# Attention block on one core: all large products of four slots in one step, all value products in the other, and result stores issued behind the copies

## What is computed

```python
xf = x.reshape(16, 1024, 512)
h = group_norm(xf, groups=32, eps=1e-6) * norm_scale + norm_bias   # mean, variance over tokens and 16 channels
q, k, v = split(h @ qkv_w + qkv_b, 3)                              # 512 x 1536
# q, k, v are reshaped (bs * 8 heads, length, 64) WITHOUT a transpose: a "head" is
# 128 consecutive tokens, and each token gives 8 positions of 64 channels (1024 positions)
a = softmax((q * s) @ (k * s).T) @ v                               # s = 64 ** -0.25, 1024 x 1024 per head
out = xf + (a.reshape(16, 1024, 512) @ proj_w + proj_b)
```

## Time and profile before

| | |
|---|---|
| median of 3 runs | 3506.1 us (3504.74 to 3506.66) |
| the profiled execution, its own time | 3506.26 us |
| its span, first to last instruction | 3504.5 us |
| VectorE busy | 2782.3 us (79%) |
| ScalarE busy | 2062.2 us (59%) |
| GpSimd busy | 1626.9 us (46%) |
| transfers | 646.87 MB, 185 GB/s; the copies' queue 76.5% of 16 engines |
| granted TensorE clock, mean | 0.998 |

### The profile page before, as it was taken

One profiled execution on the slowest core, in us unless ns is written; L12 is line 12 of the kernel. 1 busy time (PEld: TensorE's weight loads), 2 busy tenths in 40 slices (PEclk: granted clock), 3 DMA queues, 4 the chain that ended last, 5 costly groups with the idle time before them and its releaser, 6 DMA issues.

```text
span 3504.5 us, 67790 instructions
## 1 busy us (share of the span) xinstructions
PE 3454.0 (99%) x24640; PEld 2515.0 (72%) x24640; DVE 2782.3 (79%) x3473; ACT 2062.2 (59%) x3985; POOL 1626.9 (46%) x2762
## 2 busy tenths in 40 slices
PE   6999999999999999999999999999999999999998
PEld 4777777777777777777777777777777777777775
DVE  4878878888788787887888788887878878888776
ACT  5566566565565665655656656556556566565563
POOL 4454444454444444444544444445454444444452
PEclk9999999999999999999999999999999999999999
DMA  4777778777787878777777787877777778777777
GB/s 126 191 182 190 187 186 191 181 190 184 187 192 182 191 181 191 186 187 189 183 190 188 182 193 179 195 183 186 190 183 190 184 187 191 181 191 185 178 180 171
DMA packets 255707, 646.87 MB, mean 185 GB/s; under 512 B 73872, under 2 KB 73872, under 8 KB 255376
## 3 DMA queue, kind: packets, MB, share of 16 engines
q1 hardware_dynamic: 254224, 638.35, 76.5%
q10 hardware_dynamic: 1152, 4.19, 0.3%
HBM read 71.84 MB, written 33.55 MB: 30 GB/s over the span
## 4 chain that ended last, share of the span: by engine, by line
PE 91%; POOL 3%; ACT 2%; DVE 1%; issue 1%; SPq 1%; DMA 0%; POOLq 0%; ACTq 0%
PE pv_ps L399 26%; PE s_ps L369 22%; PE c_ps L439 7%; PE c_ps L440 6%; PE c_ps L441 6%; PE c_ps L422 4%; PE c_ps L450 4%; PE c_ps L452 3%; PE c_ps L424 3%; PE c_ps L423 3%; PE c_ps L451 3%; PE pv_ps L380 2%; PE s_ps L472 2%; ACT staged L519 1%; ACT probs L501 1%
## 5 line engine op out<-in xcount | busy, mean ns | idle before, releaser
L632 DVE TENSOR_REDUCE neg_max<-s_ps 128x1 f32<-128x1024 f32 x1024 | 1204.6, 1218 | 642.0 <-PE s_ps L369 642.0
L501 ACT ACTIVATE probs<-s_ps,neg_max 128x1024 f32<-128x1024 f32 x1024 | 1143.6, 1117 | 938.8 <-DVE neg_max L632 935.4
L615 DVE STREAM_TRANSPOSE turned<-probs 128x1024 f32<-128x1024 f32 x1024 | 1231.2, 1226 | 40.5 <-ACT probs L501 6.0
L399 PE MATMUL pv_ps<-probs_t,v 128*64 128x256 f32 x8192 | 999.9, 386 | 9.6 <-DMA probs_t<-turned 9.6
L399 PEld LDWEIGHTS pv_ps<-probs_t,v 128*64 128x64 f32 x8192 | 544.6, 137 | 347.0 <-issue 117.6
L439 PE MATMUL c_ps<-h_hi,w_hi 128*128 128x256 f32 x2048 | 606.7, 296 | 10.3 <-POOL h_lo L742 6.4
L440 PE MATMUL c_ps<-h_lo,w_hi 128*128 128x256 f32 x2048 | 579.3, 283 | 0.0
L441 PE MATMUL c_ps<-h_hi,w_lo 128*128 128x256 f32 x2048 | 579.1, 283 | 0.0
L519 ACT ACTIVATE staged<-c_ps,qk_bias 64x256 f32<-64x256 f32 x1024 | 479.7, 468 | 18.2 <-PE c_ps L441 4.7
L439 PEld LDWEIGHTS c_ps<-h_hi,w_hi 128*128 128x128 f32 x2048 | 391.1, 191 | 102.6 <-issue 96.6
L755 POOL CAST qh_e<-staged 128x256 fp32r<-128x256 f32 x256 | 102.4, 400 | 648.8 <-ACT staged L519 648.8
(11 more groups left out here) (71 smaller groups left out, 5171.3 us busy)
## 6 DMA issues: line engine op xcount, KB each, us to landing
probs_t<-turned SPq DMA_DIRECT2D x4096, 128.0 KB, 2.3
x_res<-in_x SPq DMA_DIRECT2D x128, 256.0 KB, 2.9
result<-x_res SPq DMA_DIRECT2D x128, 256.0 KB, 2.0
x_next<-in_x SPq DMA_DIRECT2D x120, 256.0 KB, 2.9
probs_t<-in_L_conv_qkv_w ACTq DMA_DIRECT2D x4, 768.0 KB, 8.7
turned<-in_x SPq DMA_DIRECT2D x4, 512.0 KB, 13.1
probs_t<-in_L_conv_proj_w ACTq DMA_DIRECT2D x4, 256.0 KB, 13.8
v_bias<-in_L_conv_qkv_b SPq DMA_DIRECT2D x1, 256.0 KB, 16.9
```

The costliest lines, as they stand in the source:

```text
L399: last = nc.tensor.matmul(pv_ps[side][CH * par:CH * (par + 1), 0, :], v_sb[:, ring_of(i, parity), CH * chunk:CH * (chunk + 1)], p_t[:, par ...
L501: nc.scalar.activation(probs[k % 2][:, :], s_ps[k % 2][:, :], ACT.Exp, bias=neg_max[:, k % 4:k % 4 + 1], accum_out=row_sum[:, (k // HALF) ...
L615: nc.vector.transpose(dst, probs[k % 2][:, :].rearrange("p (k b j) -> p k b j", k=CHUNKS, b=QUADS)).then_inc(probs_turned, 1)
L632: nc.vector.tensor_reduce(neg_max[:, k % 4:k % 4 + 1], s_ps[k % 2][:, :], AX.X, ALU.max, negate=True).then_inc(max_ready, 1)
```

## The change

Numbers of lines in the text are those of the kernel before. The change:

- TensorE: steps take turns. In a step with k % 4 == 0: scores of two slots, all large units of four slots (`LARGE`), the inverse transposes (`SPREAD_LAG` 8). In the other: scores of two slots and all 32 value matmuls (`ATTEND_LAG` 10). The small work stands before the third large unit (`SMALL_BEFORE`), that of slot 46 behind the value matmuls.
- The large work is laid out anew: both value units at m = 0; query/key, projection, query/key at 4 and 12; four query/key units at 8. The query/key units come in the order of tiles 0, 1, 4, 5, 2, 3, 6, 7 (0 to 3 queries, 4 to 7 keys). Statistics slots move to multiples of four.
- ScalarE, VectorE and GpSimd take their work in the new order. GpSimd runs one block of work for four slots, with `widen_inverse` of the current half as its last item but one.
- SyncE: `store` moves from m = 4 and 12, ahead of `move_half`, to m = 6 and 14, behind it. In both kernels SyncE issues it.

```diff
-STAT_SLOTS = [1, 9, 13, 17, 25, 29, 37, 41]
-STAT_STEPS = [4, 12, 14, 20, 28, 30, 38, 42]
+STAT_SLOTS = [4, 8, 12, 20, 24, 28, 36, 40]
+STAT_STEPS = [8, 12, 20, 24, 28, 36, 40, 42]
 AGGREGATE_SLOT = 42
-GROUP_MEAN_SLOT = 45
-GROUP_VAR_SLOT = 47
-AFFINE_SLOT = 47
-SPLIT_SLOT = 2
+GROUP_MEAN_SLOT = 44
+GROUP_VAR_SLOT = 46
+
+LARGE = {0: [("v", 0), ("v", 1)], 4: [("qk", 0), ("proj", 0), ("qk", 1)],
+         8: [("qk", 2), ("qk", 3), ("qk", 4), ("qk", 5)], 12: [("qk", 6), ("proj", 1), ("qk", 7)]}
+QK_TILES = [0, 1, 4, 5, 2, 3, 6, 7]
+SMALL_BEFORE = 2
 MOVE_LAG = 4
-WIDEN_LAG = 7
-ATTEND_LAG = 9
+SPREAD_LAG = 8
+ATTEND_LAG = 10
 EVAC_LAG = 12
...
@@ sync
             def slot(b, k):
-                if k == 0:
-                    load_x_tile(b, 0)
-                if k % 16 == 4:
-                    store(b, 2 * (k // 16) - 2)
-                if k % 16 == 12:
-                    store(b, 2 * (k // 16) - 1)
                 if k % HALF == MOVE_LAG % HALF:
                     move_half(b, k)
+                if k % 16 == 6:
+                    store(b, 2 * (k // 16) - 2)
+                if k % 16 == 14:
+                    store(b, 2 * (k // 16) - 1)
                 if k % 16 == 7:
                     load_residual(b, 2 * (k // 16) - 1)
                 if k % 16 == 15:
                     load_residual(b, 2 * (k // 16))
+                if k == 1:
+                    load_x_tile(b, 0)
                 if k - 2 in STAT_SLOTS[:-1]:
                     load_x_tile(b, STAT_SLOTS.index(k - 2) + 1)
...
@@ tensor
-                if k % 2 == 0 and k > 0 and small_taken(b, k - 1)[0]:
-                    pe.wait_ge(*small_taken(b, k - 1)[1:])
+                if k >= 2 and small_taken(b, k - 2)[0]:
+                    pe.wait_ge(*small_taken(b, k - 2)[1:])
...
                 if not before_start(b):
-                    pe.wait_ge(probs_ready, SPB * b + k)
+                    pe.wait_ge(probs_ready, SPB * b + k + 1)
...
-            def slot(b, k):
+            def step(b, k):
                 s = SPB * b + k
-                if k % 2 == 0 and within(s, N_SLOTS):
+                if within(s, N_SLOTS):
                     scores(b, k)
                     scores(b, k + 1)
-                large(b, k)
-                small(b, k)
-                if k % HALF == ATTEND_LAG % HALF and within(s - ATTEND_LAG, N_SLOTS):
-                    spread_inverse(b, k)
-                    attend(b, k, 0)
-                if k % HALF == (ATTEND_LAG + 2) % HALF and within(s - ATTEND_LAG - 2, N_SLOTS):
-                    attend(b, k - 2, 1)
+                if k % HALF == 0:
+                    for i, (kind, n) in enumerate(LARGE[k % 16]):
+                        if i == SMALL_BEFORE:
+                            small(b, k)
+                        make[kind](b, k, i, n)
+                    if within(s - SPREAD_LAG, N_SLOTS):
+                        spread_inverse(b, k)
+                else:
+                    if within(s - ATTEND_LAG, N_SLOTS):
+                        attend(b, k)
+                    small(b, k)
...
@@ scalar
                 if within(s, N_SLOTS):
                     softmax_exp(b, k)
+                if k % 16 == 8:
+                    stage_qk(b, k, 0)
+                if within(s, N_SLOTS):
                     softmax_exp(b, k + 1)
-                if small_unit(k + 1)[0] == "stats" and within(b + 1, BATCHES):
-                    copy_x(b, k + 1)
-                for slot in (k, k + 1):
-                    kind, n, _ = large_unit(slot)
-                    if kind == "qk" and within(made_pair(b, slot), N_PAIRS):
-                        stage_qk(b, slot, n)
+                if k % 16 == 4 or k % 16 == 12:
+                    stage_qk(b, k, 0)
+                if small_unit(k)[0] == "stats" and within(b + 1, BATCHES):
+                    copy_x(b, k)
+                if k % 16 == 4 or k % 16 == 12:
+                    stage_qk(b, k, 2)
+                if k % 16 == 8:
+                    stage_qk(b, k, 1)
+                    stage_qk(b, k, 2)
+                    stage_qk(b, k, 3)
                 if k % 16 == 0 and within(made_pair(b, k), N_PAIRS):
                     norm_x(b, k, 0)
                     norm_x(b, k, 1)
...
@@ vector
                 if within(s, N_SLOTS):
                     turn(b, k)
-                kind, _, part = large_unit(k + 1)
-                if kind == "v" and large_unit(k + 1)[1] == 1:
-                    take_v(b, k + 1)
-                if kind == "proj":
-                    take_proj(b, k + 1)
+                if k % 16 == 0:
+                    take_v(b, k, 0)
                 if within(s, N_SLOTS):
                     turn(b, k + 1)
+                if k % 16 == 0:
+                    take_v(b, k, 1)
+                if k % 16 == 4 or k % 16 == 12:
+                    take_proj(b, k, 1)
...
@@ gpsimd
             def widen_inverse(b, k):
-                n = (k - WIDEN_LAG) // HALF
+                n = k // HALF
...
-            def slot(b, k):
+            def four_slots(b, k):
                 m, pair = k % 16, k // 16
-                if k % HALF == (EVAC_LAG + 1) % HALF:
-                    split_attn(b, (k - 1) // HALF - EVAC_LAG // HALF)
-                if m == SPLIT_SLOT and within(made_pair(b, k), N_PAIRS):
-                    split_h(b, k)
-                kind, n, _ = large_unit(k)
-                if kind == "qk" and within(made_pair(b, k), N_PAIRS):
-                    split_qk(b, k, n)
-                if k % HALF == WIDEN_LAG % HALF:
-                    widen_inverse(b, k)
-                if k == AFFINE_SLOT and within(b + 1, BATCHES):
-                    affine(b)
-                if m == 9:
-                    add_bias(b, 2 * pair - 1)
-                if m == 1:
-                    add_bias(b, 2 * pair - 2)
+                if m == 4 or m == 12:
+                    split_qk(b, k, LARGE[m][0][1])
+                if m == 8:
+                    split_qk(b, k, LARGE[m][0][1])
+                    split_qk(b, k, LARGE[m][1][1])
+                split_attn(b, (k - EVAC_LAG) // HALF)
+                if m == 0:
+                    add_bias(b, 2 * pair - 2)
+                if m == 0 and within(made_pair(b, k), N_PAIRS):
+                    split_h(b, k)
+                if m == 8:
+                    add_bias(b, 2 * pair - 1)
+                if m == 4 or m == 12:
+                    split_qk(b, k, LARGE[m][2][1])
+                if m == 8:
+                    split_qk(b, k, LARGE[m][2][1])
+                    split_qk(b, k, LARGE[m][3][1])
+                widen_inverse(b, k)
+                if k == GROUP_MEAN_SLOT and within(b + 1, BATCHES):
+                    affine(b)
```

More of the change, by code:

```diff
@@ L387, in attend @@
                 i, parity = (n // 2) % 2, (n // 4) % 2
[L388 to L395, removed]
+                for quad in range(QUADS):
+                    pe.wait_ge(moved[n % 2][quad], 64 * (BLOCKS * b + n // 2 + 1))
+                if n % 4 == 0:
+                    pe.wait_ge(v_ready, 2 * (PPB * b + n // 4) + 1)
+                if n % 4 == 2:
+                    pe.wait_ge(v_ready, 2 * (PPB * b + n // 4) + 2)
+                for kt in range(8):
                     chunk = 2 * (kt % 4) + kt // 4
@@ new lines, in attend, with project @@
+                last.then_inc(pv_done, 1)
+            def project(b, k, i, n):
+                h, c = proj_block(b, k, n), bank(k, i)
+                if not within(h, N_BLOCKS):
+                    return
+                if h == 0:
+                    pe.wait_ge(w_ready, 2 * KT)
+                pe.wait_ge(attn_ready, 2 * h + 2)
+                await_bank(pe, b, k, i)
+                for j in range(KT):
+                    a_hi = attn_hi[:, j // 2, (j % 2) * P:(j % 2 + 1) * P]
+                    a_lo = attn_lo[:, j // 2, (j % 2) * P:(j % 2 + 1) * P]
+                    nc.tensor.matmul(c[:, :], a_hi, pw_hi[:, j, :], start=(j == 0), stop=False)
+                    nc.tensor.matmul(c[:, :], a_hi, pw_lo[:, j, :], start=False, stop=False)
+                    last = nc.tensor.matmul(c[:, :], a_lo, pw_hi[:, j, :], start=False, stop=(j == KT - 1))
+                last.then_inc(proj_full, 1)
@@ new lines, in make_qk @@
+            def make_qk(b, k, i, n):
+                g, c, tile = made_pair(b, k), bank(k, i), QK_TILES[n]
+                if not within(g, N_PAIRS):
+                    return
+                if before_start(b) and n == 0:
+                    pe.wait_ge(w_ready, KT)
+                await_bank(pe, b, k, i)
+                for t in range(KT):
+                    if n == 0 and t % 2 == 0:
+                        pe.wait_ge(h_split, 2 * g + t // 2 + 1)
+                    wh, wl = (w[:, t, tile * P:(tile + 1) * P] for w in (w_hi, w_lo))
+                    nc.tensor.matmul(c[:, 0:2 * P], wh, h_hi[:, t, :], start=(t == 0), stop=False)
+                    nc.tensor.matmul(c[:, 0:2 * P], wh, h_lo[:, t, :], start=False, stop=False)
```

(25 more changed lines are left out.)

137 lines of the change are left out of this document (39 added, 98 removed).

## The result

The changed kernel takes 3676.3 us (3674.3 to 3678.9, four runs) against 3506.1: ratio 1.049, interval 1.047 to 1.051. It is slower by 4.9%; 3668 was forecast. Its profiled execution has a span of 3672.6 us.

The account below looks back on a forecast made before the run. Bound: TensorE's matmuls and the changes between its kinds of work. Sum: 3506.3 - 97 + 139 + 26 + 30 + 31 + 12 + 18 + 3 = 3668 us; own range 3610 to 3730, eight in ten 3565 to 3757.

Parts of the forecast that it names:

- The forecast case: The whole kernel: all terms summed come to 3668 us, 4.6% slower; chance 0.56, own range 3610 to 3730.
- Changes removed: TensorE: two fewer changes between kinds of work in each of 256 halves, 0.19 us each, 97 us less.
- The wait at m = 8: Held GpSimd delays ScalarE's third staging, then exponentials and TensorE's scores: 2.19 us in 63 of 64 pairs, 139 us more.
- T: Start of the inverse transposes at the end of step m = 8; scores forecast at T + 7.28, without the wait T + 5.52.
- The bank at m = 4: The second query/key unit waits for the first's bank: 0.3 us in 45 places, 0.7 in 18, 26 us more.
- Once for an image: Statistics at slot 42 (30), affine work behind the held widening (31), variance product behind slot 46's values (12): about 73 us more.
- The clock: TensorE's granted clock falls behind one long stall in six, 1.7 us each: 18 us more, bounds 0 and 107.
- SyncE: SyncE's moved stores: copies start about 1 us late at most twice a pair, covered by slack; 0 us.
- Start and tail: First scores start 0.8 us earlier, last copies come some 3 us later; 3 us more.

Follow-up runs that it names:

- run 3: Run 1's kernel, with ScalarE staging the first query/key unit of m = 4 and 12 between its two exponentials; 3443.1 us, ratio 0.982.
- run 6: Run 3's kernel with the inverse transposes between the two halves of the value matmuls (lag 6), six changes in four slots instead of four; 3512.5 us, ratio 1.002.
- run 1: The changed kernel with SPREAD_LAG 4 instead of 8, so the inverse transposes come four slots earlier; 3469.7 us, ratio 0.990.
- run 2: The changed kernel with ScalarE's third and fourth staging of m = 8 moved behind the exponentials of slots 10 and 11; 3516.2 us, ratio 1.003.
- run 8: The changed kernel with one more GpSimd operation, its result unused, right behind the widening's wait in each half; 3708.6 us, ratio 1.058.
- run 5: The kernel before with only its stores moved to m = 6 and 14, behind the copies; 3513.6 us, ratio 1.0025.
- run 4: The changed kernel with SyncE's stores back at m = 4 and 12, ahead of the copies; 4016.5 us, ratio 1.146.
- run 7: Run 3's kernel with SyncE's stores back at m = 4 and 12, ahead of the copies; 3907.3 us, ratio 1.115.

## Why the prediction was right

The forecast case came in, with its mechanism: 3668 against 3676.3, 162 us added against 170. Point by point:

- **Changes removed, -97.** In run 3 an image takes 210.3 us, of which 1.7 are waits at slots 44 and 46; without them 208.6 against 214.8 before. 6.2 x 16 = 99. The neighbours that no row had shown behave like the others: transposes to scores 0.31 (1720.62 to 1720.93), where transposes to values had 0.34, and a score block ahead of values 1.60 (1720.93 to 1722.53), where one ahead of large work had 1.59. That the 99 are changes and nothing else is inferred from this; run 6, which put two back elsewhere, lost 69.
- **The wait at m = 8, +139.** By the forecast the scores come at T + 7.28, the trace has T + 7.31. Step 10 is 1.80 longer than in run 1. Steps 12 and 28 are 0.42 longer, the forecast's 0.43, and step 60, without an image tile, 0.55; taking 0.55 for slot 44 too, 32 x 2.22 + 31 x 2.35 = 144. Runs 1, 2 and 8 cut it at its first link, cut it at its second, and lengthened it, and the time followed.
- **The bank at m = 4, +26.** 24 step by step (run 3), at the forecast's 0.3 and 0.7 us. The working did not give these two: 6.45 less 5.9 and 6.3 is 0.55 and 0.15, and the 0.15 that brings them to 0.7 and 0.3 stands nowhere in it. That they fit is partly luck.
- **Once for an image, +73.** Measured over their neighbours: slot 44 1.80 (2.0 was forecast), slot 46 0.93 (0.8), slots 50 and 52 0.55 + 1.30 (2.1): 4.58 x 15 = 69. Slot 44, which has no image tile, is held against slot 60, the other step at m = 12 without one: 9.96 against 8.16. In it TensorE waits 1.10 us for the bank, the wait that the forecast names.
- **The clock, +18.** It fell to 0.50 in 14 of the steps at m = 12. At slot 28 such a step took 9.94 instead of 8.45 (six times), at slot 60 9.51 instead of 8.15 (four), at slot 12 of the last image 9.50, where slot 28 of that image took 8.15: 16 us in all. Two falls at slot 44 cost nothing, since the step waits for its bank anyway (9.96 with and without), and the one in the first image has no neighbour to be held against. So the sum fits, but by two errors that cancel: more falls than the guessed one in six, and less for each than 1.7. The long stall alone did not bring the clock down, in 49 of 63 it did not; where the fall came, 1.73 us was the longest gap (timeline above). The falls lie in the same slot of images in a row, slot 60 of images 1 to 4 and slot 28 of 6 to 10 (images counted from 0); what picks the place stays open. The Trainium skill (page "TensorE: Matmul & The Clock Gate", section "Why this matters for your kernels") warns only of idle gaps longer than this one; the trace does not agree in 14 cases of 63.
- **SyncE, 0.** Right for the sum: steady steps without the waits above are as forecast. But the sentence that this part of the change does nothing was the weakest: in the old order it is worth next to nothing (8 us lost, run 5), and it is what keeps the new order from losing another 340 us (run 4; 464 in run 7). Of the queue I had costed the copies and the residual, not the tile load between them, though the order of the code shows it.
- **Start and tail, +3.** First scores come at 58.5 instead of 56.2 us, where 0.8 earlier was forecast; the last pair and tail take 6.4 us more, the first image 5 more than the others do: 14, the term that was worst. No run shows why.

Sum of the measured: -99 + 144 + 24 + 69 + 16 + 14 = 168, and the profiled spans differ by 168.1. Most of the terms are medians times a count, so they are not as exact as the sum looks.

## What to carry to other kernels

Count what a reordering removes from the busiest engine, and then walk each helper's queue in its new order: a small operation that waits for the big engine (here a copy of 0.4 us with one buffer) holds everything behind it, and its price is paid where a third engine has queued its own urgent work behind the result. A stall of this kind shows in the waits as an engine with a low busy share that is released by the very engine that it serves. Where such a wait is found, try the lag or the order of the queue first: one constant gave back 207 us here, and the order of a queue decided 464.

## What was not expected

- The place of two stores in a queue of transfers that is 77% busy was worth 340 and 464 us, the most of any edit here, while the same move in the kernel before cost 8.
- Two changes between kinds of matmuls cost 0.39 us where they were removed (99 us over 256 halves) and 0.27 where they were put back around the inverse transposes (69 us).
- The granted clock fell behind 14 of 63 stalls of the same length (1.73 us) in the changed kernel, and behind 26 where the stall was 0.34 us longer (run 8; mean granted clock 0.982 to 0.985 in its four executions against 0.989 to 0.990). At slot 44 such a fall cost nothing, because TensorE waits there anyway.
